# A two-layer graph attention kernel on one core: two y products swap PSUM banks, and the gate row c goes over the partitions through DRAM

## The reference, cut to what matters

```
Q, K, V = x @ W_q + b_q, x @ W_k + b_k, x @ W_v + b_v         # 8 heads of 64
a = x @ w_g[:D];  c = x @ w_g[D:]
scores = Q K^T / 8 + (a[:, :, None] + c[:, None, :] + b_g + log(adj + 1e-9))
x1 = softmax(scores) V + x                                     # layer 0
q, k = x1 @ Wq + bq, x1 @ Wk + bk
att = softmax(where(adj == 0, -1e18, q k^T / sqrt(512))), masked entries 0
out = layernorm(x1 + (att @ x1) @ Wc) * gamma + beta           # layer 1
```

## Time and profile before

| what | value |
| --- | --- |
| median of 3 runs | 2406.81 us |
| the profiled execution, its own time | 2408.92 us |
| its span in the trace | 2407.1 us |
| mean granted TensorE clock | 0.992 |
| PE busy | 2321.3 us, 96% |
| DVE busy | 1754.0 us, 73% |
| ACT busy | 1219.3 us, 51% |
| POOL busy | 894.4 us, 37% |
| DMA | 253.26 MB, mean 105 GB/s, 32.2% of the 16 engines in the main queue |

### The profile page before, as it was taken

The page is one execution under the profiler, slowest core; times in us unless marked ns, Lnnn a source line. Parts: engine busy times, 40 slices in busy tenths (PEclk is TensorE's granted clock), DMA queues, the critical chain, the costliest instruction groups (busy, mean ns, idle before and its releaser), DMA issues.

```text
span 2407.1 us, 39433 instructions
## 1 busy us (share of the span) xinstructions
PE 2321.3 (96%) x13520; PEld 1898.1 (79%) x13520; DVE 1754.0 (73%) x5476; ACT 1219.3 (51%) x3474; POOL 894.4 (37%) x1146
## 2 busy tenths in 40 slices
PE   7999999999999999999999999999999999999985
PEld 5778888788888788888788887788887888887774
DVE  4667777777777677777777776777776777776766
ACT  4454455555455544445544455544545554555442
POOL 0243334443334433334433344432344433344423
PEclk9999999999999999999999999999999999999997
DMA  6223333323333323333323333233333233333221
GB/s 233 93 88 110 105 101 115 119 84 103 113 106 106 118 93 96 111 114 106 107 96 101 102 127 106 91 107 106 102 118 115 84 106 110 105 110 115 75 70 45
DMA packets 155768, 253.26 MB, mean 105 GB/s; under 512 B 17072, under 2 KB 99120, under 8 KB 151344
## 3 DMA queue, kind: packets, MB, share of 16 engines
q1 hardware_dynamic: 155568, 250.75, 32.2%
HBM read 150.02 MB, written 100.66 MB: 104 GB/s over the span
## 4 chain that ended last, share of the span: by engine, by line
PE 95%; DVE 3%; ACT 1%; SPq 1%; DMA 0%; issue 0%; POOL 0%; DVEq 0%
PE bank L206 27%; PE bank L208 25%; PE bank L207 25%; PE bank L437 6%; PE bank L450 5%; PE bank L473 5%; DVE y_lo L1061 1%; ACT y_hi L748 1%; PE bank L367 1%; PE bank L482 1%; PE bank L421 1%; DVE x1n L1000 0%; DMA x1n<-in_wkT 0%; DVE bnst L1070 0%; DVE x1n L1067 0%
## 5 line engine op out<-in xcount | busy, mean ns | idle before, releaser
L1204 POOL TENSOR_TENSOR probs<-probs,rcp 128x512 f32<-128x512 f32 x256 | 261.2, 1040 | 1294.7 <-DVE rcp L942 1294.7
L714 ACT ACTIVATE probs<-probs,nmax 128x128 f32<-128x128 f32 x1024 | 397.3, 391 | 196.4 <-DVE nmax L932 196.4
L1000 DVE STREAM_TRANSPOSE x1n<-x1T 32x512 f32<-32x512 f32 x512 | 359.9, 703 | 116.9 <-DMA out<-x1n 109.8
L206 PE MATMUL bank<-x_hi,wk_hi 128*128 128x512 f32 x512 | 209.9, 410 | 50.0 <-DVE y_lo L1061 42.3
L735 ACT ACTIVATE g_sb<-bank,consts 128x512 f32<-128x512 f32 x128 | 88.0, 688 | 316.5 <-PE bank L208 314.7
L932 DVE CUSTOM_DVE_ANT_0 probs<-bank,bias 128x128 f32<-128x128 f32 x1024 | 227.6, 287 | 1.5 <-issue 0.2
L703 ACT ACTIVATE q_sb<-bank,consts 128x512 f32<-128x512 f32 x128 | 88.0, 688 | 274.3 <-PE bank L208 274.3
L1212 POOL TENSOR_TENSOR x_lo<-xT_land,x_hi 128x512 fp32r<-128x512 f32 x124 | 169.5, 1396 | 148.8 <-ACT x_hi L668 148.8
L206 PE MATMUL bank<-x_hi,wm_hi 128*128 128x512 f32 x512 | 206.0, 402 | 9.7 <-DVE x_lo L964 9.7
L951 DVE STREAM_TRANSPOSE turned<-probs 128x1024 f32<-128x1024 f32 x128 | 158.7, 1240 | 71.5 <-POOL probs L1204 67.3
L206 PE MATMUL bank<-x_hi,wq_hi 128*128 128x512 f32 x512 | 208.7, 408 | 0.0
(11 more groups left out here) (128 smaller groups left out, 5339.8 us busy)
## 6 DMA issues: line engine op xcount, KB each, us to landing
turn_dram<-turned SPq DMA_DIRECT2D x128, 512.0 KB, 2.6
probsT<-turn_dram SPq DMA_DIRECT2D x512, 128.0 KB, 2.8
out<-x1n SPq DMA_DIRECT2D x128, 256.0 KB, 3.2
xn<-in_x SPq DMA_DIRECT2D x126, 256.0 KB, 2.7
xT_land<-in_xT SPq DMA_DIRECT2D x31, 1024.0 KB, 6.4
adj_sb<-in_adj SPq DMA_DIRECT2D x32, 256.0 KB, 3.3
v_sb<-in_wk SPq DMA_DIRECT2D x4, 256.0 KB, 5.4
xT_land<-in_xT SPq DMA_DIRECT2D x4, 256.0 KB, 5.6
```

What stands on the lines that cost most here:

```text
L206: nc.tensor.matmul(out_ap, st[0], mv[0], start=start, stop=False)
L714: op = nc.scalar.activation(probs[:, k, :], probs[:, k, :], ACT.Exp, bias=nmax[:, k:k + 1], scale=-1.0, accum_out=sums[:, k:k + 1])
L1000: op = nc.vector.transpose(x1n[b * BLK:(b + 1) * BLK, :, :] .rearrange("p g (c a s) -> p a c g s", c=C, a=P // BLK)[:, a, :, :, :], x1T[a ...
L1204: nc.gpsimd.tensor_tensor(probs[:, half, :], probs[:, half, :], rcp[:, half].unsqueeze(2).to_broadcast([P, HALF, P]), ALU.mult)\
```

## The change

Two things are changed. The y product 2 goes to bank 1 and the y product 3 to bank 0, where it was the other way round; the waits of the products that write these banks afterwards are exchanged to match. And `gate_rows` goes: the 128x4 tile `c_c` is stored to DRAM by SP, read back as one row of 512 numbers broadcast to 128 partitions (`c_rows`, graph index innermost, so that a graph's 128 numbers stand 4 apart), and `bias` reads it there in place of bank 7. PE's waits that came with bank 7 change too.

```
@@ the bank of a y product
-            return bank[((4, 5, 2, 3) if last else (2, 3, 0, 1))[g]]
+            return bank[((4, 5, 2, 3) if last else (2, 3, 1, 0))[g]]
@@ SP, new, called behind the first xn loads of step 0 and behind move_probs(t, 2) of each step that has a next
+            def spread_c(t):
+
+                sp.wait_ge(s["dve_a"], nth("dve_a", t, 3))
+                sp.dma_start(c_dram, c_c[:, :]).then_inc(s_cst0, 16)
+                sp.wait_ge(s_cst0, 16 * (t + 1))
+                if t > 0:
+                    sp.wait_ge(s["dve_b"], nth("dve_b", t - 1))
+                sp.dma_start(c_rows[:, :], c_dram.rearrange("(o j) g -> o (j g)", o=1).to_broadcast([P, P * GG]))\
+                    .then_inc(s_crow, 16)
@@ PE, chunk 3 of the first step's weight product
-                else:
-                    pe.wait_ge(s["dve_b"], 1)
@@ PE, gone
-            def gate_rows(t):
-
-                pe.wait_ge(s["dve_a"], nth("dve_a", t, 3))
-                for g in range(GG):
-                    mm = nc.tensor.transpose(bank[7][:, g * P:(g + 1) * P],
-                                             c_c[:, g:g + 1].to_broadcast([P, P]), ident[:, :])
-                mm.then_inc(s["pe_cb"], 1)
@@ PE, yw(2) and yw(3)
-                        pe.wait_ge(s["act_q"], nth("act_q", t, 3))
-                    else:
                         pe.wait_ge(s["act_k"], nth("act_k", t, 3))
+                    else:
+                        pe.wait_ge(s["act_q"], nth("act_q", t, 3))
@@ PE, the seam
-                    pe.wait_ge(s["dve_y"], nth("dve_y", w, 3))
+                    pe.wait_ge(s["dve_y"], nth("dve_y", w, 2))
                 project_k(t, 0)
                 if w >= 0:
                     context_rest(w)
-                    pe.wait_ge(s["dve_tp"], nth("dve_tp", w))
-                else:
-                    pe.wait_ge(s_lo["m"], 4)
-                gate_rows(t)
-                if w >= 0:
-                    pe.wait_ge(s["dve_y"], nth("dve_y", w, 2))
+                if w >= 0:
+                    pe.wait_ge(s["dve_y"], nth("dve_y", w, 3))
                 project_q(t, 0)
@@ PE, before pv(u, 3)
-                pe.wait_ge(s["dve_b"], nth("dve_b", t))
+                if w >= 0:
+                    pe.wait_ge(s["dve_tp"], nth("dve_tp", w))
+                else:
+                    pe.wait_ge(s_lo["m"], 4)
@@ DVE, bias
-                dve.wait_ge(s["pe_cb"], nth("pe_cb", t))
+                dve.wait_ge(s_crow, 16 * (t + 1))
                 dve.wait_ge(s["act_ln"], nth("act_ln", t))
+                c_row = c_rows[:, :].rearrange("p (j g) -> p g j", g=GG)
-                    op = nc.vector.scalar_tensor_tensor(out=bias0[:, g, :], in0=bank[7][:, g * P:(g + 1) * P],
+                    op = nc.vector.scalar_tensor_tensor(out=bias0[:, g, :], in0=c_row[:, g, :],
@@ DVE, the first gate of a step
+                    dve.wait_ge(s_cst0, 16 * t)
```

More of the change, by code:

```diff
@@ L97, in gnn_program @@
         ln_adj = sb("ln_adj", [P, GG, P])
+        c_rows = sb("c_rows", [P, P * GG])
         bias0 = sb("bias0", [P, GG, P])
@@ L131, in gnn_program @@
         bank = [ctx.enter_context(nc.psum_tensor(f"bank{i}", [P, 512], f32)) for i in range(8)]
-        PER = dict(pe_q=4, pe_k=4, pe_cb=1, pe_s=8, pe_v=4, pe_pv=4, pe_g=4, pe_sa=4,
+        PER = dict(pe_q=4, pe_k=4, pe_s=8, pe_v=4, pe_pv=4, pe_g=4, pe_sa=4,
                    pe_y=4, pe_tp=1, pe_ctx=4,
@@ L149, in gnn_program @@
         s_pw = [sem(f"turned_stored{c}") for c in range(C)]
+        s_cst0 = sem("c_stored")
+        s_crow = sem("c_rows_loaded")
+        c_dram = nc.dram_tensor("c_dram", (P, GG), f32, kind="Internal").ap()
         PT_MOVES = P // BLK
@@ L315, in body @@
                 else:
+                    spread_c(0)
                     sp.wait_ge(s_lo["q"], C)
@@ L341, in body @@
                     move_probs(t, 2)
+                    if it.nxt:
+                        spread_c(t + 1)
                 if last:
@@ L502, in layer1_alone @@
                     else:
-                        pe.wait_ge(s["dve_y"], nth("dve_y", w, c))
+                        pe.wait_ge(s["dve_y"], nth("dve_y", w, 5 - c))
                     g_part(c, 0)
@@ L544, in first_step @@
                 m_chunk(0)
-                gate_rows(0)
                 scores(0, 0)
@@ L589, in yw @@
                     elif g == 2:
+                        pe.wait_ge(s["act_k"], nth("act_k", t, 3))
+                    else:
                         pe.wait_ge(s["act_q"], nth("act_q", t, 3))
-                    else:
-                        pe.wait_ge(s["act_k"], nth("act_k", t, 3))
                     hi_lo(y_bank(g, False)[:, :], act_rows(x1_hi, x1_lo, g), w_rows("c")).then_inc(s["pe_y"], 1)
                 if w >= 0:
-                    pe.wait_ge(s["dve_y"], nth("dve_y", w, 3))
+                    pe.wait_ge(s["dve_y"], nth("dve_y", w, 2))
                 else:
```

## The result

The changed kernel takes 2380.44 us (median of 4 runs, 2379.4 to 2381.6) against 2407.35 (4 runs) of the kernel before: a ratio of 0.9887, 95% interval 0.987 to 0.9904, so 26.9 us faster. Forecast were 2376 and a range of 2340 to 2394. The profiled execution has 2379.4 us, its span 2377.6 us, granted clock 0.991.

A forecast was written before the change was run, and what follows sets the result against it. PE was taken as the bound (95% of the chain of waits), stalling at seams. Terms -51.3 - 14.6 + 34.5 + 1 = -30.4 us gave 2378.5 from the profiled 2408.9, 2376 on the runs' scale; range 2340 to 2394.

The forecast's parts named there:

- The bank swap: At project_k, PE's wait for the low part of y goes: 1.71 us at each of 30 seams, 51.3 us removed.
- The transposes: Behind the context matmuls, PE's four transposes of c go: 0.47 us in each of 31 steps, 14.6 us removed.
- What is late next: With PE 2.18 us earlier, scores(t, 0) holds by 0.4 us; project_v(t, 1) has 1.04 us slack, behind the bias on DVE.
- The bias from SBUF: POOL's gamma_b and beta_b hold DVE's bias, so project_v(t, 1) stalls 1.15 us at 30 seams: +34.5 us, bounds 0 and 63.
- The spread through DRAM: Store and broadcast load of c at the seam: c_rows is there 3.5 us before the bias, no cost.
- The first step: In step 0, c_rows lands at 35.4 behind full queues and delays the bias: +1 us, bounds 0 and 10.
- Rival 1: At the bias, the shared port costs nothing on the path; 0.7 us late, inside the slack: 2342 us; chance 0.20.
- rival 2: At bias(t), c_rows lands late, 8.1 us per transfer, losing 4.4 us net per seam: 2539 us; chance 0.06.
- rivals 3 and 4: At project_k, y_low(2) ends late and k waits 0.5 us (2394), or something else holds k (2393); together 0.10.

The follow-up runs named there:

- moving POOL: Changed kernel with POOL's affine(w, 0) moved behind sigma(w, 2) and sigma(w, 3): 2349.24 us, ratio 0.9755 against the kernel before.
- the residual moved alone: Changed kernel with residual1(w, 3) placed ahead of bias(t) on DVE: 2349.89 us, ratio 0.9756 against the kernel before.
- the faster version: Changed kernel with residual1(w, 3) ahead of bias(t), and c through transposes and bank 7 in step 0 only: 2341.67 us, ratio 0.9728 against the kernel before.
- the packed rows: Changed kernel with the c row stored and loaded graph by graph, a graph's 128 numbers side by side: 2556.6 us, ratio 1.0619 against the kernel before.

## Why the prediction was right, step by step

**The bank swap: 51.3 us forecast, 51.5 measured alone.** Right in kind and size (1.71 us a seam forecast and measured); the stall went wholly, as the 1.0 us to spare for y_low(2) said.

**The transposes: 14.6 us.** Right: 0.47 us a step forecast, 0.47 measured with the spread alone. The version without step 0's loss and without the new stall should be at 2407.2 - 51.3 - 14.6 = 2341.3, and it measures 2341.7.

**What is late next.** Right as to the place, which is project_v(t, 1) and not scores(t, 0), and as to what stands in front of it, the bias.

**The bias from SBUF: 3.1 us forecast, 3.12 measured; the stall 34.5 us forecast, 31 measured** (31.2 and 30.5 in the two kernels that take it away in different ways, 1.03 a step). The hold by POOL's gamma_b and beta_b is shown by moving POOL, and it went as the forecast had it, the first and the second held. The restart of 0.14 us that I added is most of the difference: the forecast had 1.01 us a seam without it. It was no new cost. In the kernel before, the v matmuls stood behind narrow score matmuls without any wait, and their second start came just as slowly (1259.07 and 1259.41 before, 1246.10 and 1246.44 now). One part of the working was off and is hidden in the sum, which is luck: the four take 1.48 us unheld and not 1.11, because of the stride. Against that, beta_b let the second go a little sooner than I had it, and the narrow POOL instructions behind it added nothing. The page "SBUF — State Buffer" of the Trainium skill, section "Who interferes with whom", says that a DVE instruction with two SBUF inputs contends with a GpSimd one that reads SBUF. The runs bear it out: 0.43 us for an instruction in POOL's pause, up to 1.43 held, and 0.34 beside the same work of POOL with one input from PSUM.

**The spread through DRAM: no cost in the steps.** Right, with other parts: the store takes 1.4 us and not 2.6, the load 4.5 and not 2.7, so the row lands 6.0 us behind the gate where 6.1 was forecast. That the two errors cancel is luck. Doubling the load cost the steps nothing (71.67 us against 71.66).

**The first step: +1 us forecast, 8 measured** (2349.89 against 2341.67). This is the mis-sized term, within its bounds of 0 and 10, and its place and mechanism were right. In step 0 of the changed kernel (DMA issues, DVE and PE, each start us and us, the idle time in brackets), to be held against the earlier trace rows:

```profile
28.17 0.43 SPq L279 DMA_DIRECT2D c_dram<-c_c  x1
33.23 0.33 SPq L283 DMA_DIRECT2D c_rows<-c_dram  x1
```

```profile
37.99 1.48 DVE L922 SCALAR_TENSOR_TENSOR bias<-c_rows,a_c,ln_adj 128x128 f32<-128x128 f32 x4 [10.21 <-issue]
```

```profile
44.86 1.48 PE L444 MATMUL bank<-k_sb,q_sb 64*128 64x128 f32 x16 [4.29 <-ACT q_sb L708]
```

The bias starts at 37.99 and not at my 35.4: the store is issued 0.9 us later than xT was, and the two transfers take 5.0 and 4.7 us where I had taken 5 and 3. The bias is 4.6 us late, and 4.1 of it reach PE: the scores start at 44.86 in place of 40.80, behind a wait of 4.3 us for q_sb in place of 0.8. I had halved it for no reason that a row gave. The clock comes on top. In this window of the changed kernel (columns as above) the granted clock is 0.79, where the kernel before had 1.00:

```profile
42.00:50.00 8.00, 5.14 (x22) 2.89 (x23) 5.18 (x22) 2.81 (x12) 2.08 (x2) 0.79 0.12 35
```

PE's timelines of the two kernels of 2349.89 and 2341.67, which differ in the first step alone, separate the parts. First the residual moved alone, then the faster version:

```profile
44.80 2.03 PE L444 MATMUL bank<-k_sb,q_sb 64*128 64x128 f32 x16 [4.60 <-ACT q_sb L708]
...
80.86 5.54 PE L404 MATMUL bank<-cols,x1n 128*128 128x1 f32 x32
```

```profile
40.96 1.16 PE L453 MATMUL bank<-k_sb,q_sb 64*128 64x128 f32 x16 [0.78 <-ACT q_sb L718]
...
75.42 3.71 PE L405 MATMUL bank<-cols,x1n 128*128 128x1 f32 x32
```

The scores come 3.8 us later, which is the wait. The v matmuls a few us behind them come 5.4 later (50.64 against 45.19), so 1.6 is the lower clock there, and it is still 5.4 at the narrow matmuls at 80.86. From these to the first q matmul of step 1, 13.4 us pass in one kernel and 10.2 in the other, with granted clocks of 0.62 and 0.83: another 3.2. This last part is not all the late row's. The same stretch takes 11.7 us in the trace of the kernel before (from 75.24) and 11.7 in that of the changed one (from 80.92), and against the trace of the kernel before the changed kernel has lost 5.7 us when it is through. But the profiled execution of the kernel before was 1.6 us above its median and that of the changed kernel 1.0 below, so the medians leave about 8 here too. What sets the length of that stretch in one execution stays open.

**The sum.** With the two removed terms as forecast and the two added ones as measured: 2407.35 - 51.3 - 14.6 + 31 + 8 = 2380.45, against 2380.44. The forecast of 2376 is nearer than its parts deserve: the stall was sized 3.5 us too dear and the first step 7 too cheap, and the two partly cancel.

**Rival 1** (the port costs nothing) falls with the 3.12 us and the wait; **rival 2** (the row is late) did not happen, but two other kernels show it: one load more costs the steps nothing, two more cost 3.5 us a step and the slow store of the packed rows 5.8, of which some 1.5 and 2.2 are not waiting but PE's lower clock; **rivals 3 and 4** (the stall comes back or stays) fall with the swap alone, whose steps are 1.71 us shorter.

## What to carry to other kernels

Moving an operand of VectorE from PSUM to SBUF can nearly triple the instructions' time when GpSimd works beside it (1.11 us to 3.12 here): look at what GpSimd does in that very microsecond, and if the instruction stands in front of something that TensorE waits for, put that something first. A change of two parts is to be run in parts, since here one of them alone beat both together by 24 us. And a detour through DRAM that is free in the steady state still had a price in the first step here, where the same store took 5.0 us in place of 1.4 and no earlier work covered it.

## What the runs showed of the hardware that I had not expected

- A VectorE scalar_tensor_tensor of 128 numbers takes 0.43 us with 16 bytes between neighbours in one SBUF operand, 0.347 packed.
- A store of 512 single 4-byte numbers from 128 partitions to DRAM takes 9.8 us, the same 2 KB as 128 pieces of 16 bytes 1.4 us.
- Behind a gap of 3.2 us TensorE was granted the lower clock for seven or eight 128x512 matmuls, from the fourth on; behind gaps of 1.0 and 1.4 us it was not. The 2.0 us of longer waiting cost 3.5 us a step.
